# Splitting the setup meeting of a graph-network kernel for Pool, with 40 dense blocks ahead of layer 1's pairs

## The reference

```
h = relu(layernorm(x))
msg = relu(h[src]) + 1e-7
ex = exp(msg - max)                      # of each destination
agg = segment_sum(msg * ex / segment_sum(ex))
out = agg + h;  h = relu(batchnorm(out @ W1 + b1)) @ W2 + b2
```

## Time and profile before

| what | us |
|---|---|
| median of 3 runs (3526.11 to 3533.01) | 3531.97 |
| the profiled execution, its own time | 3531.61 |
| its span | 3529.8 |
| PE busy of the span | 3096.0 (88%) |
| POOL busy of the span | 2379.9 (67%) |
| DVE busy of the span | 2047.2 (58%) |
| ACT busy of the span | 1871.0 (53%) |
| POOL scatters (L681) x508 | 493.3 |
| POOL gathers of the three layers (L666), the group of pair_rings x728 | 730.6 |
| mean granted clock of PE | 0.937 of 2.4 GHz |

### The profile page before, as it was taken

How to read it: one execution, slowest core, us unless ns; L and a number is a source line. 1 busy time by engine, 2 the same in 40 slices (tenths; PEclk the granted TensorE clock), 3 DMA queues, 4 the chain that set the end, 5 groups by cost and what they waited for, 6 DMA issues and landing times.

```text
span 3529.8 us, 67853 instructions
## 1 busy us (share of the span) xinstructions
PE 3096.0 (88%) x19129; PEld 2552.0 (72%) x19129; DVE 2047.2 (58%) x4862; ACT 1871.0 (53%) x3489; POOL 2379.9 (67%) x2488
## 2 busy tenths in 40 slices
PE   2799995069998789999789999876999999999998
PEld 0466663058887777887777888765888888888887
DVE  7665552025455556455566554674666767767665
ACT  0432221056665677665578666564555555555554
POOL 3777777746777355777455777626777777777773
PEclk7799997589999899999889999987999999999998
DMA  9586553068888467888556888657555666556662
GB/s 342 179 282 223 184 181 103 0 226 262 279 280 264 138 219 235 279 275 270 169 185 231 273 277 273 219 149 203 156 162 164 165 164 165 167 163 164 166 164 82
DMA packets 419112, 713.33 MB, mean 202 GB/s; under 512 B 75586, under 2 KB 259068, under 8 KB 416099
## 3 DMA queue, kind: packets, MB, share of 16 engines
q1 hardware_dynamic: 270119, 323.69, 30.4%
q0 software_dynamic: 130688, 321.08, 30.3%
q10 hardware_dynamic: 18107, 66.24, 5.0%
HBM read 561.35 MB, written 149.39 MB: 201 GB/s over the span
## 4 chain that ended last, share of the span: by engine, by line
PE 58%; POOL 19%; issue 8%; DVE 6%; ACT 3%; DMA 3%; ACTq 2%; SPq 1%; DVEq 1%; POOLq 0%
POOL pair_rings L666 12%; PE ps L1596 11%; PE ps L2242 5%; PE ps L2281 5%; PE ps L2263 5%; PE ps L2275 5%; PE ps L2292 5%; PE ps L728 4%; PE ps L716 3%; PE ps L734 3%; POOL adjacency L681 3%; PE ps L2244 3%; PE ps L1619 3%; PE ps L720 3%; POOL end_rows L666 2%
## 5 line engine op out<-in xcount | busy, mean ns | idle before, releaser
L2232 POOL DMA_INDIRECT ring<-h_table,idx_ring x832 | 806.2, 969 | 259.7 <-issue 231.2
L1596 PE MATMUL ps<-casts,two_parts 128*128 128x500 f32 (+1 forms) x3464 | 780.1, 380 | 199.4 <-DVE two_parts L1686 185.8
L666 POOL DMA_INDIRECT pair_rings<-split_table,src_idx x728 | 730.6, 1004 | 288.3 <-issue 216.0
L1596 PEld LDWEIGHTS ps<-casts,two_parts 128*128 128x128 f32 x3464 | 626.8, 192 | 315.9 <-DVE two_parts L1686 188.1
L681 POOL DMA_INDIRECT adjacency<-edge_counts,places_of_counts x508 | 493.3, 971 | 202.7 <-issue 152.2
L1492 ACT ACTIVATE casts<-spare 128x1000 fp32r<-128x1000 fp8e4 (+1 forms) x471 | 459.0, 974 | 10.6 <-DMA spare<-adjacency 7.0
L1686 DVE TENSOR_TENSOR two_parts<-work,two_parts 128x512 fp32r<-128x512 f32 (+1 forms) x276 | 187.4, 679 | 435.5 <-ACT two_parts L1482 435.3
L2329 ACT ACTIVATE work<-acc,vecs 128x512 f32<-128x512 f32 x208 | 150.3, 723 | 388.7 <-DVE acc L2386 330.2
L1482 ACT ACTIVATE two_parts<-work 128x512 fp32r<-128x512 f32 (+1 forms) x276 | 170.3, 617 | 268.8 <-PE ps L1596 256.7
L1471 ACT ACTIVATE work<-work,negc 128x256 f32<-128x256 f32 x300 | 149.1, 498 | 271.0 <-DMA work<-msg_table 147.3
L2281 PEld LDWEIGHTS ps<-mats,work 128*128 128x128 f32 x1664 | 217.8, 191 | 100.4 <-issue 100.4
(11 more groups left out here) (329 smaller groups left out, 6159.2 us busy)
## 6 DMA issues: line engine op xcount, KB each, us to landing
spare<-adjacency SPq DMA_DIRECT2D x216, 250.0 KB, 4.3
acc<-e_few SPq DMA_DIRECT2D x208, 256.0 KB
work<-msg_table SPq DMA_DIRECT2D x144, 256.0 KB, 4.8
work<-in_edge_attr SPq DMA_DIRECT2D x104, 256.0 KB
e_few<-spare SPq DMA_DIRECT2D x52, 512.0 KB
spare<-rel_rows SPq DMA_DIRECT2D x208, 84.0 KB
spare<-adjacency SPq DMA_DIRECT2D x72, 187.5 KB, 4.2
e_few<-work SPq DMA_DIRECT2D x26, 512.0 KB
```

The costliest lines, as they stand in the source:

```text
L666: e.indirect_dma_start(out=to, out_offset=None, in_=table, in_offset=bass.IndirectOffsetOnAxis(ap=src_idx[:, 2 * i + h, j:j + 1], axis=0)) ...
L1596: ins = e.matmul(bank, parts_of(d)[:, b % 2, q, kind * D:(kind + 1) * D], cast_counts[n % CASTS][:, at:at + width], start=opens, stop=(b = ...
L2232: e.indirect_dma_start(out=rows[:, s, j, :], out_offset=None, in_=h_table, in_offset=bass.IndirectOffsetOnAxis(ap=idx_ring[:, s, j:j + 1], ...
```

## The change

The setup's Pool program is cut in two. Pool does 384 of its 508 scatters (`EARLY`), then drains and reports at the meeting, and does the other 124 between its report and its wait for the other engines. The other four engines can pass when all have reported. The wait for the scatters moves from Pool to SP and is made by region: for the first 384 before the first counts are loaded, for all before the counts of region 2. The wait for the split table moves to SP's end of the setup. `few_e0` becomes a semaphore that isn't cleared between phases. In layer 1 (layer index 0), 40 blocks of region 0 have steps -8 to -1, five a step, ahead of the first pair; the remaining 156 blocks are spread evenly by columns over the 42 steps, 3 or 4 a step in regions 0 to 2 and 4 or 5 in region 3. `JOBS` becomes a list for each layer: layer 1's W1 jobs of region 0 move from steps 10 to 13 to steps 5 to 8, and others by a few steps. The lists of the two later layers and the jobs after the last pair (`LATE`, `TAIL`) are what they were. `need` has one more condition, that the last segment's edges begin at or past region 2. The diff, cut to its core:

```diff
+EARLY = 384
+LEAD = 8
+LEAD_BLOCKS = 40
-def step_of(n):
+def step_of(layer, n):
     r, b = divmod(n, BLOCKS)
     columns = [sum(widths) for _, widths in REGIONS]
     before = sum(BLOCKS * w for w in columns[0:r]) + b * columns[r]
+    if layer == 0:
+        lead = sum(columns[k // BLOCKS] for k in range(LEAD_BLOCKS))
+        if n < LEAD_BLOCKS:
+            return n * LEAD // LEAD_BLOCKS - LEAD
+        return (before - lead) * PAIRS // (BLOCKS * sum(columns) - lead)
...
-        def scatters(e, S):
-            for i in range(COLS):
+        def scatters(e, S, first, end):
+            for i in range(first, end):
...
-                    reached(e, S("few_e0"), 2 * pairs_behind(n))
+                    reached(e, S("lasting_few_e0"), 2 * pairs_behind(n))
...
-        def scattered(e, S):
+        def scattered(e, S, end):
             for b in range(SCATTERS):
-                e.wait_ge(S(f"gather_spread{b}"), 16 * EACH * len(range(b, COLS // EACH, SCATTERS)))
+                e.wait_ge(S(f"gather_spread{b}"), 16 * EACH * len(range(b, end // EACH, SCATTERS)))
...
                     attributes_sync(e, S)
+                    split_stored0(e, S)
...
                 e.wait_ge(S("addresses"), 1)
-                scatters(e, S)
-                scattered(e, S)
-                split_stored0(e, S)
+                scatters(e, S, 0, EARLY)
+
+            def pool_past_arrival(e, S):
+
+                if not again:
+                    scatters(e, S, EARLY, COLS)
...
+                    if ready and d == 2 * DUOS:
+                        scattered(e, S, COLS)
...
                 for j in range(2):
                     load_dense_rows(j)
+                if ready:
+                    scattered(e, S, EARLY)
                 for d in range(3):
                     load_counts(d)
...
-                for i in range(-1, PAIRS + 3):
+                for i in range(-lead - 1, PAIRS + 3):
...
-                for i in range(PAIRS + 3):
-                    blocks = [n for n in range(ALL_BLOCKS) if step_of(n) == i]
+                for i in range(-lead, PAIRS + 3):
+                    blocks = [n for n in range(ALL_BLOCKS) if step_of(layer, n) == i]
...
-            def meet():
+            def meet(past_arrival, S):
 
                 met[0] += 1
                 e.drain()
                 e.sem_inc(bar, 1)
+                if past_arrival is not None:
+                    past_arrival(e, S)
                 e.wait_ge(bar, 5 * met[0])
                 e.drain()
...
+    need[0, GROUP0 + (SEGMENTS - 1) * WIDE // J] = CUT + REGIONS[2][0]
```

More of the change, by code:

```diff
@@ L96, in step_of, with blocks_halfway @@
     return FIRST_STEPS + (before - first) * (PAIRS - FIRST_STEPS) // (BLOCKS * sum(columns) - first)
-def blocks_halfway(i):
-    steps = [step_of(n) for n in range(BLOCKS * len(REGIONS))]
+def blocks_halfway(layer, i):
+    steps = [step_of(layer, n) for n in range(BLOCKS * len(REGIONS))]
     return sum(s < i for s in steps) + sum(s == i for s in steps) // 2 if i in steps else 0
@@ L133, in stored_duos, with dense_jobs @@
     return 16 * (d // STORED + 1)
-def dense_jobs():
+def dense_jobs(layer):
     jobs = [(pairs_of(c) + 3, c * CH, pairs_of(c), True) for c in range(CUT // CH)]
@@ L143, in dense_jobs @@
             for n in range(width // CH):
-                jobs.append((step_of(BLOCKS * (r + 1) - 1) + 3, CUT + at + n * CH, chunks, False))
+                jobs.append((step_of(layer, BLOCKS * (r + 1) - 1) + 3, CUT + at + n * CH, chunks, False))
             at += width
-    out, now = [], -1
+    out, now = [], -LEAD - 1
     for ready, node, least, sparse in sorted(jobs):
@@ L150, in dense_jobs @@
     return out
-JOBS = [j for j in dense_jobs() if j[0] < PAIRS - 1]
-LATE = [j for j in dense_jobs() if j[0] >= PAIRS - 1]
+JOBS_OF = [[j for j in dense_jobs(layer) if j[0] < PAIRS - 1] for layer in range(L)]
+LATE = [j for j in dense_jobs(0) if j[0] >= PAIRS - 1]
 FIRST_OF_LAST = CHUNKS - len(REGIONS[-1][1]) + 1
@@ L159 @@
         [(node, least, sparse) for _, node, least, sparse in LATE if sparse and least == PAIRS]]
-NJOBS = len(JOBS) + len(LATE)
+NJOBS = len(JOBS_OF[0]) + len(LATE)
 MATS = ["nw0", "few1", "fnw0", "fnw1", "fnw2", "nw2", "nw1", "ew0", "ew1", "ew2", "few0_e0", "few0_e1", "few0_h"]
@@ L656, in attributes_sync, with pair_gathers @@
                 e.wait_ge(S(f"term_out{b}"), 16 * (NPAIR // 4))
-        def pair_gathers(e, S, i, raw):
+        def pair_gathers(e, S, layer, i, raw):
             b = slot_of(i)
@@ L661, in pair_gathers @@
                 if h == 1:
-                    reached(e, S("dense"), blocks_halfway(i - 1))
+                    reached(e, S("dense"), blocks_halfway(layer, i - 1))
                 for j in range(J):
@@ L697, in step @@
                     for t in range(2):
-                        wait(e, S("few_e0"), k, 2, t + 1)
+                        wait(e, S("lasting_few_e0"), k, 2, t + 1)
                         if t == 0:
@@ L733, in step @@
                         half = slice(t * HALF, (t + 1) * HALF)
-                        e.matmul(ps[2 + t][:, :], few0_e[t][half, :], er0T[b][half, :, :], start=True, stop=True).then_inc(S("few_e0"), 1)
+                        e.matmul(ps[2 + t][:, :], few0_e[t][half, :], er0T[b][half, :, :], start=True, stop=True).then_inc(S("lasting_few_e0"), 1)
             pipeline(e, NPAIR, SLOTS, SLOTS, 1, step)
@@ L839, in step @@
                     wait(e, S("e0T"), i)
-                    wait(e, S("few_e0"), i - SLOTS, 2)
+                    wait(e, S("lasting_few_e0"), i - SLOTS, 2)
                     e.tensor_scalar(er0T[b], ps[7][:, :].rearrange("p (j c) -> p j c", c=HALF), 0.0, None,
@@ L1012, in setup_phase @@
                 names += ("zero_fill zero_fill_rest addresses hit counted bad bad_row worse issued e0 e0T er erT onehot sums agg0 "
-                          "few_e0 term ea0 ea1 ea2 ea3 term_out0 term_out1 term_out2 term_out3 rows_in0 rows_in1 rows_in2 rows_in3 "
+                          "term ea0 ea1 ea2 ea3 term_out0 term_out1 term_out2 term_out3 rows_in0 rows_in1 rows_in2 rows_in3 "
                           "v_exp v_mul v_high v_low split_out0 split_out1").split()
-            return ("setup", names, dict(sync=sync, pool=pool, act=act, pe=pe, dve=dve))
+            return ("setup", names, dict(sync=sync, pool=pool, pool_past_arrival=pool_past_arrival, act=act, pe=pe, dve=dve))
         phases.append(setup_phase(False))
@@ L1321, in edges_phase @@
             columns = iota_w[:, :]
+            lead = LEAD if ready else 0
+            JOBS = JOBS_OF[layer]
             by_node = [work[0:WW, b, 0:2 * D] for b in range(2)]
@@ L1367, in duos_at @@
             def duos_at(i):
-                return [d for d in range(ALL_DUOS) if step_of(first_block(d)) == i + 1]
+                return [d for d in range(ALL_DUOS) if step_of(layer, first_block(d)) == i + 1]
             def blocks_of(u):
@@ L1381, in evacuated @@
             def evacuated(i):
-                return [r for r in range(len(REGIONS)) if step_of(BLOCKS * (r + 1) - 1) + 1 == i]
+                return [r for r in range(len(REGIONS)) if step_of(layer, BLOCKS * (r + 1) - 1) + 1 == i]
             def jobs_of(i):
@@ L1444, in pool @@
                         split_stored(e, S, range(STORED))
-                    pair_gathers(e, S, i, raw)
+                    pair_gathers(e, S, layer, i, raw)
             def act(e, S):
@@ L2833, in run @@
                         parts[who](e, S)
-                    meet()
+                    meet(parts.get(who + "_past_arrival"), S)
                     done.append((used, len(done) % 2))
```

## The result

| | before | after |
|---|---|---|
| median of the runs | 3531.33 us (4 runs, 3526.11 to 3533.01) | 3490.79 us (4 runs, 3487.84 to 3492.73) |
| ratio | | 0.9892, 95% interval 0.9881 to 0.9904 |
| the profiled execution, own time | 3531.61 | 3487.84 |
| its span | 3529.8 | 3486.0 |
| mean granted clock | 0.937 | 0.946 |

The change brings 40.5 us, 33.3 were forecast, and the time lies within the stated range. The profiled execution happens to be the fastest of the four runs of after; the end of the phase, where ACT begins the nodes of layer 1, moved by 38.2 us (1215.47 to 1177.27).

A forecast was written before the change was run, and what follows sets the result against it. Bound: a hole with only Pool working from 600 to 700 us, then PE up to pair 9, then Pool. Drains +4.3, scatters +3.5, pairs -37.8, tail -3.3 sum to -33.3: 3498.5 us forecast, range 3485 to 3517.

The forecast's parts named there:

- The hole and the lead: Behind setup's meeting: first dense matmul at 607.3 us, lead ends at 682, step 0's blocks at 689, all 40 blocks hidden.
- The drains: Pool's two drains, at its report and after the last scatter: 6.3 us each, +6.0 and -1.75, net +4.3 us.
- The scatters: About 97 of Pool's scatters run beside dense work at +43 ns each: +3.5 us, bounds 0 and 4.2.
- Rival C: DVE's two-operand work stops Pool's scatters in full: +22 us in place of +3.5, 3517 us; chance 8%.
- The pairs: Layer 1, first gather to pair 41's: Pool runs without a stall at 10.46 us a pair, -37.8 us.
- The tail: Behind Pool's last gather in layer 1: PE's sum of pair 40 begins earlier, tail 3.3 us shorter, bounds 0 and 5.
- The range's own terms: Drain -4.3 to +3.5, scatters -3.5, tail +3.3 and half of B's gathers, said to reach 3485 to 3508 us.
- B: With fewer blocks beside them gathers come near 957 ns, a pair takes 10.06 us: -50, 3482 us; chance 7%.
- D: PE keeps the pace in part: Pool's gates or PE's buffer waits cost 0.4 us a pair, 3515 us; chance 9%.
- E: Steps 1 to 41: PE's idling lowers its granted clock; ten steps at 1.2 GHz give +37, 3569 us; chance 4%.

## Why the prediction was right

Point by point, by the profiled executions:

- **The hole and the lead: right.** First dense matmul at 600.8 (forecast 607), lead and step 0 done at 682.5 (forecast 689): all 40 blocks lie in the hole. The lead without the split shows what the cover is worth: 84.9 us of stall. The forecast's start was 6 us too late: DVE's wait for the copy of Z0 fell from 21.1 to 16.9 us, and the meeting opened at 579.4, 1.5 earlier.
- **The drains: mis-sized.** Forecast net +4.3, with 6.3 us for each. Measured 4.64 at the report and 3.77 at the last scatter, so the second gap won back what the first cost: +4.3 - 4.3 = 0. The waits for the landing in the old gap of 8.05 aren't the whole reason. The two kernels that report behind all 508 scatters have no such wait on Pool, and their gap is still 6.52 (shown for the lead without the split), near my 6.3. Why a drain in the split meeting costs less than that no run shows.
- **The scatters: right in kind, low in size.** 3.5 forecast; the 124 took 5.5 more, at +45 ns each (43 forecast, for fewer of them). With the report 0.9 later in this execution the first gather came at 715.8 (forecast 717.1). Rival C's cause, DVE's two-operand work, is the right one, as cutting that work showed; its price of 22 is not, because Pool stands only where one of its DMAs begins within such an operation, which 11 of the 124 did.
- **The pairs: right.** Forecast -37.8; measured 427.3 (1143.17 - 715.83) against 466.5, so -39.1. Pool had no stall and 10.42 us a pair (10.46 forecast). The split alone takes the startup stall away, the lead the 3.2 us in pairs 5 to 8.
- **The tail: low.** Forecast -3.3; measured 29.9 - 23.6 = 6.3 (1177.27 - 1153.69). PE's sum of pair 40 began at 1145.31, 8.4 before Pool's end (7.0 forecast), and step 41 has four blocks in place of five, 1.4 us, which I hadn't looked up; I had said that region 3 stays as it was.
- **Sum:** first gather +6.5, pairs -39.1, the last pair 0.8 longer, tail -6.3: -38.2, against -33.3. What failed in size is the drain term (by 4.3) and the tail (by 3.0), both to the same side; the scatters' 2.0 went against them. The remaining 5.6 us between the two profiled executions lie behind layer 1, in phases that the change leaves alone (2314.3 us before, 2308.7 after). They are within the spread of 2307.2 to 2314.5 that the ten traces with this code show, so of the median's 40.5 some 2 us are luck of the executions, and the 36.7 on another chip fits that. The range's own terms, added up, reach from 3482 to 3505 and not from 3485 to 3508; 3490.8 lies within both.
- **The rivals.** B (gathers back to 957 ns by themselves) didn't come: they stayed at 999. C: above. D didn't come: no wait of Pool for PE. E, the clock: it was granted at 0.96 from 810 to 1154 and not near 1.00 as I had said, with PE waiting for rows in half of the steps and not in nearly every one. That cost nothing, since Pool never waited.

## What to carry to other kernels

Where one engine alone is late to a meeting, let it report early and go on, and give the others work that doesn't need the rest; but size that work by the hole, since in the open the same 40 blocks cost some 50 us. Then find the engine that is the chain from there on and work on its own instructions: here a drain and another engine's operands were worth more than further blocks. Half the lead was nearly as good as all of it, because slack on PE buys nothing once Pool has no stall. And don't price an interference by the busy time of the engine that causes it: only the DMAs that began within one of its operations paid here.

## What the runs showed of the hardware

- A drain on Pool behind an indirect DMA kept the next one back. In the five traces with a split meeting and its drains the gap was 3.55 to 5.01 us at the report and 3.76 or 3.77 behind the last scatter, in the two that report behind all 508 it was 6.52, and in the kernel before, with a wait for the landing ahead of the drain, 8.05. Without a drain it was 0.30 us.
- A Pool indirect DMA that began while a DVE operation with both operands in SBUF was under way took longer (32 gathers with 0.2 us or more of a low part to run: 1.25 us on the average against 0.95). One that began beside a DVE reciprocal, with one operand, didn't (37 gathers, 0.95 at most). DVE's low parts kept their 0.69 us in either order.
- Moving one small operand (84 columns) of a 0.8 us operation to PSUM left DVE's time at 798 ns and took 29 ns off the mean gather, 18 us off the kernel.
- The granted clock of PE was 0.87 of 2.4 GHz from 716 to 810, behind 41 us without work, and 0.96 from 810 to 1154, with waits for rows of up to 4.0 us; it had been 1.00 from 842 to 1186 in the kernel before.
